# A gated pair of 3x3 convolutions on TensorE's four row groups: contiguous runs of 57 columns a slot, nine-slot blocks, and a new order of visits

## The reference

```python
def qconv_cg(x, w, theta):
    base = cin // 4
    yp = conv3x3(x[:, :base], w[:, :base])
    yr = conv3x3(x[:, base:], w[:, base:])
    d = sigmoid(2.0 * (yp - theta))
    return yp + d * yr
h = relu(bn(qconv_cg(x, w_a, theta_a), ...a))
h = bn(qconv_cg(h, w_b, theta_b), ...b)
return relu(x + h)
```

## Time and profile before

| | |
|---|---|
| median of 3 runs | 467.6 us (467.1 to 467.66) |
| the profiled execution's own time | 467.52 us |
| its span, first to last instruction | 465.7 us |
| TensorE busy | 452.9 us (97%) |
| VectorE, ScalarE busy | 256.0 us (55%), 222.1 us (48%) |
| matmuls | 8233, 8208 of them L323 |

### The profile page before, as it was taken

The page is one execution under the profiler, slowest core; times in us unless marked ns, Lnnn a source line. Parts: engine busy times, 40 slices in busy tenths (PEclk is TensorE's granted clock), DMA queues, the critical chain, the costliest instruction groups (busy, mean ns, idle before and its releaser), DMA issues.

```text
span 465.7 us, 17751 instructions
## 1 busy us (share of the span) xinstructions
PE 452.9 (97%) x8233; PEld 444.1 (95%) x8233; DVE 256.0 (55%) x423; ACT 222.1 (48%) x348; POOL 6.9 (1%) x20
## 2 busy tenths in 40 slices
PE   4999999999999999999999999999999999999994
PEld 4899999999999999999999999999999999999993
DVE  6316655565655565555656565555555565555553
ACT  5226645454544545454544444454545454434332
POOL 5000000000000000000000000000000000000000
PEclk9999999999999999999999999999999999999997
DMA  9930000801526051080605342080333003012315
GB/s 166 219 57 1 4 4 1 140 3 30 114 43 100 4 121 21 4 141 6 136 3 99 45 98 45 3 140 3 67 76 65 9 3 72 1 23 51 72 37 104
DMA packets 116394, 27.13 MB, mean 58 GB/s; under 512 B 116192, under 2 KB 116192, under 8 KB 116320
## 3 DMA queue, kind: packets, MB, share of 16 engines
q1 hardware_dynamic: 115408, 25.86, 30.1%
q10 hardware_dynamic: 592, 0.13, 0.1%
q0 software_dynamic: 320, 0.00, 0.0%
HBM read 13.14 MB, written 12.85 MB: 56 GB/s over the span
## 4 chain that ended last, share of the span: by engine, by line
PE 95%; DMA 2%; ACT 1%; DVE 1%; issue 0%; ACTq 0%
PE acc L323 94%; DMA out_dram<-rows_out 1%; PE acc L287 1%; DMA w_nat<-in_L_conv_w_a_dram 1%; DVE rows_out L545 0%; ACT rows_out L441 0%; ACT L422 0%; ACT mix L422 0%; DVE w_pad L460 0%; ACT w_hi L380 0%; DVE mix L524 0%; ACT x_hi L395 0%; DVE w_pad L458 0%; ACTq L414 0%
## 5 line engine op out<-in xcount | busy, mean ns | idle before, releaser
L323 PE MATMUL acc<-h_hi,w_hi 32*128 32x448 f32 x1392 | 226.7, 367 | 0.0
L323 PE MATMUL acc<-h_lo,w_hi 32*128 32x448 f32 x1392 | 226.6, 367 | 0.0
L323 PE MATMUL acc<-h_hi,w_lo 32*128 32x448 f32 x1392 | 226.5, 367 | 0.0
L323 PE MATMUL acc<-x_hi,w_hi 32*128 32x448 f32 x1344 | 224.4, 374 | 0.8 <-ACT w_hi L380 0.8
L323 PE MATMUL acc<-x_lo,w_hi 32*128 32x448 f32 x1344 | 224.0, 373 | 0.0
L323 PE MATMUL acc<-x_hi,w_lo 32*128 32x448 f32 x1344 | 223.9, 373 | 0.0
L323 PEld LDWEIGHTS acc<-h_hi,w_hi 32*128 32x128 f32 x1392 | 188.3, 184 | 1.2
L323 PEld LDWEIGHTS acc<-h_hi,w_lo 32*128 32x128 f32 x1392 | 188.2, 183 | 1.2
L323 PEld LDWEIGHTS acc<-h_lo,w_hi 32*128 32x128 f32 x1392 | 188.2, 183 | 1.0
L323 PEld LDWEIGHTS acc<-x_hi,w_hi 32*128 32x128 f32 x1344 | 185.5, 188 | 2.7 <-ACT x_hi L395 1.4
L323 PEld LDWEIGHTS acc<-x_hi,w_lo 32*128 32x128 f32 x1344 | 185.8, 188 | 1.3
(11 more groups left out here) (48 smaller groups left out, 30.3 us busy)
## 6 DMA issues: line engine op xcount, KB each, us to landing
x<-in_x_dram SPq DMA_DIRECT2D x30, 392.0 KB, 5.6
out_dram<-rows_out SPq DMA_DIRECT2D x30, 392.0 KB, 6.8
out_dram<-rows_out SPq DMA_DIRECT2D x5, 112.0 KB, 2.5
x<-in_x_dram SPq DMA_DIRECT2D x1, 280.0 KB, 4.8
x<-in_x_dram SPq DMA_DIRECT2D x1, 266.0 KB, 5.5
w_nat<-in_L_conv_w_a_dram SPq DMA_DIRECT2D x1, 144.0 KB, 3.0
w_nat<-in_L_conv_w_b_dram SPq DMA_DIRECT2D x1, 144.0 KB, 4.5
x<-in_x_dram ACTq DMA_DIRECT2D x1, 126.0 KB, 3.1
```

Source lines behind the costliest of these rows:

```text
L323: return pe.matmul(psum[:, bank, 0:N], w[g * ROWS:(g + 1) * ROWS, tap], moving(blk, part, c, dx, g), start=(u == 0 and g in (0, 1)), stop= ...
```

## The change

The moving tiles get a pitch of 57 (`PITCH`): one column of zeros stands between two slots and serves both. A matmul then reads one contiguous run over all slots of its block, the zero columns with it, and their sums are left unread in PSUM. An 8-slot block has 456 columns (`leading` 1), a 9-slot block 512 (`leading` 0, a bank). An a block that takes four slots of each of two images has two runs of 228. The b blocks have nine slots, 12 of them and one of eight slots for each ring of four images, so there are 52 b blocks, 48 with nine slots. Total: 108 blocks.

The order of visits is new. Four blocks are a round; groups 1, 2 and 3 go through its blocks in different turns (`TURNS`) and start 0, 6 and 12 steps after each other, group 0 starts 20 steps after group 1 (`OFFSET`). The first group in a block waits for the inputs and the bank, each later one for the group before it in that block (`group_before`, `visit_done`). There are 18 x 108 + 20 = 1964 steps. ScalarE and VectorE no longer do one block after another but a written order over the round. A b block goes at least eight places (`MARGIN`) behind the a block it needs, as long as a blocks are left; `order` begins with nine a blocks and ends with eight b blocks. The transposes of layer b's weights come before step 13 and those of the parameters before step 16, and six chunks of `x` are split before the loop instead of four.

```diff
-BLK = 8
+BLK, BLK_B = 8, 9
 YR_BANKS, YP_BANKS = 5, 3
-LAG = (42, 0, 21, 42)
+ROUND = 4
+TURNS = ((0, 1, 2, 3), (0, 3, 2, 1), (1, 0, 3, 2), (2, 1, 0, 3))
+OFFSET = (20, 0, 6, 12)
+FIRST_GROUP = (1, 2, 3, 1)
+LAST_GROUP = (3, 1, 2, 3)
 XH_IMGS, X_IMGS, H_IMGS, OUT_IMGS, MIX = 4, 6, 4, 2, 4
-AHEAD = 4
+MARGIN = 8
+AHEAD, SOON = 6, 4
...
-    PADW = W + 2
-    N = BLK * W
+    PITCH = W + 1
     HALF = BLK // 2
...
-    NA, NB = B // 2 * A_PAIR, B * XS // BLK
-    LEAD = A_PAIR
-    order = [("a", n) for n in range(LEAD)]
-    for n in range(max(NA - LEAD, NB)):
-        if n < NB:
...
+    NA = B // 2 * A_PAIR
+    b_blocks = [(ring * HRING + t, min(BLK_B, HRING - t))
+                for ring in range(B // H_IMGS) for t in range(0, HRING, BLK_B)]
+    NB = len(b_blocks)
...
+    order, place = [], {}
+    for n in range(NA + NB):
+        na = sum(kind == "a" for kind, m in order)
+        nb = len(order) - na
+        ready = nb < NB and na >= a_needed(nb) and place["a", a_needed(nb) - 1] + MARGIN <= n
+        blk = ("b", nb) if na == NA or ready and order[-1][0] == "a" else ("a", na)
+        place[blk] = n
+        order.append(blk)
+    TOTAL = len(order)
+    assert TOTAL % ROUND == 0
...
+    def visits(g, b):
+        return b // ROUND * ROUND + TURNS[g].index(b % ROUND) + 1
+    def group_before(g, b):
+        if g in (0, FIRST_GROUP[b % ROUND]):
+            return None
+        return g - 1 if g > 1 else GROUPS - 1
...
+    def slots_of(blk):
+        kind, n = blk
+        return b_blocks[n][1] if kind == "b" else BLK
+    def leading(blk):
+        return 0 if slots_of(blk) == BLK_B else 1
...
-        x_hi = sb("x_hi", [P, XH_IMGS, XS, PADW], F32R)
-        x_lo = sb("x_lo", [P, XH_IMGS, XS, PADW], F32R)
-        h_hi = sb("h_hi", [P, HRING + 1, PADW], F32R)
-        h_lo = sb("h_lo", [P, HRING + 1, PADW], F32R)
-        mix = sb("mix", [P, MIX, N])
+        x_hi = sb("x_hi", [P, XH_IMGS, 1 + XS * PITCH + 1], F32R)
+        x_lo = sb("x_lo", [P, XH_IMGS, 1 + XS * PITCH + 1], F32R)
+        h_hi = sb("h_hi", [P, 1 + (HRING + 1) * PITCH + 1], F32R)
+        h_lo = sb("h_lo", [P, 1 + (HRING + 1) * PITCH + 1], F32R)
+        mix = sb("mix", [P, MIX, BLK_B * W])
...
+        def rows_of(bank, blk):
+            first, k = bank * BANK, slots_of(blk)
+            if leading(blk):
+                at = psum_flat[:, first:first + k * PITCH]
+            elif bank:
+                at = psum_flat[:, first - 1:first - 1 + k * PITCH]
+            else:
+                return psum_flat[:, 0:k * PITCH].rearrange("p (s w) -> p s w", w=PITCH)[:, :, :W]
+            return at.rearrange("p (s w) -> p s w", w=PITCH)[:, :, 1:]
...
-                nc.gpsimd.memset(t[:, :, 0:PADW:PADW - 1].bitcast(F32), 0.0).then_inc(hpads_zero, 1)
+                nc.gpsimd.memset(t[:, 0:1].bitcast(F32), 0.0)
+                nc.gpsimd.memset(t[:, 1::PITCH].bitcast(F32), 0.0).then_inc(hpads_zero, 1)
...
                 kind, n = blk
                 rows = slice(g * ROWS, (g + 1) * ROWS)
+                back = 1 - leading(blk)
                 if kind == "a":
                     tile = (x_hi, x_lo)[part]
                     parts = a_slots(n)
                     img, s, k = parts[0]
-                    at = img % XH_IMGS
+                    at = back + (s + c) * PITCH + dx
                     if len(parts) == 1:
-                        return tile[rows, at, s + c:s + c + k, dx:dx + W]
-                    return tile[rows, at:at + 2, s + c:s + c + k, dx:dx + W]
-                tile = (h_hi, h_lo)[part]
-                t = BLK * n % HRING
-                if t == HRING - HALF:
-                    halves = tile[rows, c:c + HRING].rearrange("p (a b) w -> p a b w", b=HALF)
-                    return halves[:, 0::HRING // HALF - 1, :, dx:dx + W]
-                return tile[rows, t + c:t + c + BLK, dx:dx + W]
+                        return tile[rows, img % XH_IMGS, at:at + k * PITCH]
+                    return tile[rows, img % XH_IMGS:img % XH_IMGS + 2, at:at + k * PITCH]
+                t, k = b_blocks[n]
+                at = back + (t % HRING + c) * PITCH + dx
+                return (h_hi, h_lo)[part][rows, at:at + k * PITCH - back]
+            def sums(bank, blk):
+                kind, n = blk
+                to = psum[:, bank, 0:slots_of(blk) * PITCH - 1 + leading(blk)]
+                if kind == "a" and len(a_slots(n)) == 2:
+                    return to.rearrange("p (i w) -> p i w", i=2)
...
-                return pe.matmul(psum[:, bank, 0:N], w[g * ROWS:(g + 1) * ROWS, tap],
+                alone = g == 0
+                return pe.matmul(sums(bank, blk), w[g * ROWS:(g + 1) * ROWS, tap],
                                  moving(blk, part, c, dx, g),
-                                 start=(u == 0 and g in (0, 1)), stop=(u == UNITS - 1 and g in (0, 3)))
-            for step in range(UNITS * TOTAL + max(LAG)):
-                if step == UNITS:
-                    weights(1, 3)
-                if step == UNITS + 2 * TAPS:
+                                 start=(u == 0 and (alone or g == FIRST_GROUP[b % ROUND])),
+                                 stop=(u == UNITS - 1 and (alone or g == LAST_GROUP[b % ROUND])))
+            for step in range(UNITS * TOTAL + max(OFFSET)):
+                if step == 13:
+                    pe.wait_ge(wlo_ready, 2)
+                    weights(1, 6)
+                if step == 16:
                     pe.wait_ge(prmdup_ready, 2)
                     pe.transpose(psum[:, 5, 0:10], prm_dup[:].rearrange("n c q -> n (c q)"),
                                  ident[0:10, 0:10]).then_inc(prmT_ready, 1)
                 for g in (1, 2, 3, 0):
-                    if not 0 <= step - LAG[g] < UNITS * TOTAL:
+                    if not 0 <= step - OFFSET[g] < UNITS * TOTAL:
                         continue
-                    b, u = divmod(step - LAG[g], UNITS)
+                    visit, u = divmod(step - OFFSET[g], UNITS)
+                    b = visit // ROUND * ROUND + TURNS[g][visit % ROUND]
                     kind, n = order[b]
-                    if g == 1 and u == 0:
...
-                                pe.wait_ge(whi_ready, 4)
-                                pe.wait_ge(wlo_ready, 4)
                         if b >= YR_BANKS:
                             pe.wait_ge(gated_ready, b - YR_BANKS + 1)
...
-                    if g in (2, 3) and u == 0:
-                        pe.wait_ge(tile_done[g - 1], b + 1)
+                    if u == 0 and group_before(g, b):
+                        pe.wait_ge(visit_done[group_before(g, b)], visits(group_before(g, b), b))
                     if g == 0 and u == 0 and b >= YP_BANKS:
                         pe.wait_ge(mixed_ready, b - YP_BANKS + 1)
-                    if g == 1 and u == 0 and b in (3, 4):
+                    if g == 0 and u == 0 and b == 0:
+                        pe.wait_ge(rvar_ready, 1)
+                    if g == 0 and u == 0 and b == 1:
                         pe.wait_ge(whi_ready, 4)
                         pe.wait_ge(wlo_ready, 4)
-                    if g == 0 and u == 0 and b == 0:
-                        pe.wait_ge(rvar_ready, 1)
                     mm = unit(g, b, u)
                     if u == UNITS - 1:
-                        mm.then_inc((yp_ready, tile_done[1], tile_done[2], yr_ready)[g], 1)
+                        mm.then_inc(visit_done[g], 1)
...
-            for n in range(1, AHEAD):
+            for n in range(1, SOON):
                 split_hi(*chunk_of(n))
-            weights_hi(1, 3)
+            weights_hi(1, 6)
             act.wait_ge(rvar_ready, 2)
             nc.scalar.activation(rstd0[:], rvar[:], ACT.Sqrt).then_inc(rstd0_ready, 1)
+            for n in range(SOON, AHEAD):
+                split_hi(*chunk_of(n))
             act.wait_ge(consts_ready, 1)
...
+            for b in range(0, TOTAL, ROUND):
+                gate(b)
+                split_ahead(b)
+                gate(b + 1)
+                split_ahead(b + 1)
+                finish(b)
+                gate(b + 2)
+                finish(b + 1)
+                finish(b + 2)
+                split_ahead(b + 2)
+                gate(b + 3)
+                finish(b + 3)
+                split_ahead(b + 3)
...
+            for b in range(0, TOTAL, ROUND):
+                split_ahead(b)
+                mix_sums(b)
+                split_ahead(b + 1)
+                mix_sums(b + 1)
+                low_parts(b)
+                mix_sums(b + 2)
+                low_parts(b + 1)
+                low_parts(b + 2)
+                split_ahead(b + 2)
+                mix_sums(b + 3)
+                low_parts(b + 3)
+                split_ahead(b + 3)
```

More of the change, by code:

```diff
@@ L514, in _, with mix_sums @@
                 nc.vector.tensor_copy(prm_dup[:, :, q], prm_rows[:]).then_inc(prmdup_ready, 1)
-            for n in range(1, AHEAD):
+            for n in range(1, SOON):
                 split_lo(*chunk_of(n))
-            weights_lo(1, 3)
```

(37 more changed lines are left out.)

141 lines of the change are left out of this document (61 added, 80 removed).

## The result

The changed kernel takes 455.98 us (median of 4 runs, 455.21 to 456.26), the kernel before 467.35 beside it (4 runs, 466.98 to 467.66). The ratio is 0.9754, interval 0.9737 to 0.9771: 11.4 us less, where 37.6 less was forecast. The profiled execution took 456.05 us, with a span of 454.2.

A forecast was written before the change was run, and what follows sets the result against it. TensorE bounds the kernel: steps times pace, plus start and tail. 7.4 + 8.0 start + 399.3 steps + 6.0 waits + 0.2 latency + 6.9 tail = 427.8, plus 1.8 outside the span: 429.6 us; range 422 to 465.

The forecast's parts named there:

- Steps, columns: TensorE's loop: 2094 steps become 1964; groups run freely, so the mean of 480.9 columns counts, 0.2004 us a step.
- The rival in step: TensorE's loop: each step lasts as its widest matmul, 512 columns nearly always; 444 us in all, chance 0.09.
- What a contiguous matmul carries: Cost of each TensorE matmul beyond its columns: 2.9 ns, between bounds 0 and 23.6, giving 0.2033 us a step.
- The text's own sign of being wrong: TensorE's matmul spacing: the prediction is wrong if 480 columns take over 0.21 us, or waits exceed 0.5 us a round.
- The low level shows no cost: Argument for 2.9 ns: at 1.2 GHz matmuls take only their columns, so the extra cost looks like feeding restarted each run.
- the cost is per matmul: Rival on TensorE's pace: the 23.6 ns is paid once per matmul, a step is 0.2240 us; 463 us, chance 0.14.
- Part of the 23.6 stays: Rival on TensorE's pace: another floor of a group's stream leaves some 12 ns a matmul; 441 us, chance 0.22.
- Waits inside a round: Faster steps make group 1 wait for a bank at a round's fourth block: 0.2 to 0.3 us a round, 6 us.
- Start: Before the loop's full pace: clock rises at 21.9 us, so the start loses 8.0 us, against 10.5 before.
- Tail: After TensorE's last unit: 6.9 us of sigmoid, VectorE, ReLU and store, unchanged because the last block keeps eight slots.
- PSUM reads at pitch 57: VectorE's reads of PSUM in rows of 56 with gaps: expected near 0.62 and 0.68 us, no slower for the gaps.
- the slower rival: Gapped PSUM reads lengthen the round's chain: each 0.1 us more costs 13 us, double length gives 510 us; chance 0.08.

The follow-up runs named there:

- the first bench: Matmuls alone, no layer computed, operand form varied by stretch; a group's starts lie 206.7 ns apart for float32r 448 in one run, 189.2 for bf16.
- the bench: Matmuls alone, float32r, several pitches, then 512 columns with and without other engines working: 226.7 ns each, 228.9 with each group's columns shifted.

## Why the prediction was wrong, point by point

**Steps, columns: right.** 1964 steps, and groups that keep each its own pace. The mean of columns is the one that counts; with the units above the mean is (60 x 208.9 + 48 x 231.4)/108 = 218.9 ns. The rival in step is refuted by the rows at 409.38 to 409.90, and by the step of 0.2206, since 512 columns and 18 ns in nearly every step would make 0.229. The Trainium skill's rule that matmuls start in program order (TensorE: Matmul & The Clock Gate, "The mechanism") doesn't hold for the starts of different row groups in this trace. For what the semaphores say it does; see the last section.

**"What a contiguous matmul carries": this step failed.** It took 2.9 ns, one run's share of 23.6; the measured value is 18.5. 1964 times the missing 15.6 is 30.6 us, and 429.6 + 30.6 = 460.2. The terms below (4 less in waits, 1.7 less at the start, 1.4 more in the tail) make it 455.9. The bounds (0 to 23.6) held it, and so did the wide range (422 to 465); the choice of 2.9 between the bounds didn't, nor did the forecast's own range (423 to 437), whose cost per matmul ended at 5 ns. The text's own sign of being wrong, 480 columns in over 0.21, came true. Two arguments carried the choice. "The low level shows no cost" was true, but a cost once per float32r matmul vanishes at that level too (in the first bench one group alone, 448 columns in one run at the 1.2 GHz level, has 373.3 ns, its columns and nothing more), so it told nothing of runs. And the one shape in the trace was read as eight equal runs, when nothing there varied the number of runs. What is there instead: 16 to 20 ns for each float32r matmul of 448 columns, 2.5 for bf16, and a few ns for where the rows start. The nearest rival, in mechanism and in time, was "the cost is per matmul", with 23.6 ns, 463 us and a chance of 0.14; with 18.5 it gives 1964 x 5.1 = 10 us less, 453, and the waits of 2 us that its slower step had ruled out. "Part of the 23.6 stays" (12 ns, 441 us, 0.22) lies 15 us off. The Trainium skill's gap of about 2.5 ns beyond the columns (the same page, "Back-to-back issue gap") fits bf16 here (189.2 for 448 columns, 2.5 beyond them) and not float32r (206.7, 20.0 beyond).

**Waits inside a round: wrong in size, and in place.** 6.0 us forecast. The text had said that above 0.213 a step the waits go; with 0.2189 about 2 remain, as 0.2206 against 0.2195 shows. Per round they are 0.08 us at the start of group 0's fourth block, which the text had called just in time, and 0.05 for groups 1 to 3, inside or at the start of the first block of their round; group 1 loses nothing at the start of its fourth block, where the 0.2 to 0.3 had been put.

**Start: right, and a little better.** Loss forecast 8.0, against 10.5 before; measured 6.3. That is what the other terms leave of TensorE's stretch (445.94 - 0.2 - 7.56 - 429.9 - 2), but a count gives the same: by 50 us group 1 has begun 172 units, 162 of them of 456 columns, worth 36.2 us at their paces, and 50 - 7.56 - 36.2 = 6.3. The high level came at 19.55, not 21.9.

**Tail: 1.4 us short.** 6.9 was carried over as unchanged, since the last block keeps eight slots; but four blocks now end nearly together and queue on VectorE.

**PSUM reads at pitch 57: right.** 644, 642 and 647 ns for (60 x 448 + 48 x 504)/108 = 473 elements on average, beside 621 and 634 for 448: the slower rival is refuted.

The sum with measured terms: 7.6 + 6.3 + 429.9 + 2 + 0.2 + 8.3 + 1.8 = 456.1, against 456.05 profiled. What tests it is the start counted at 50 us; taken as the remainder, it would make the sum agree by itself.

Where the gain of 11.4 us comes from, by kernels that differ in one part: pitch 57 gives 4.3 with runs (0.9909) and 5.5 with rows (0.9882); the nine-slot blocks with the new start's transposes, on top of the runs, 1.7; the new order 5.2. The nine-slot blocks cut the fixed 18.5 ns to fewer matmuls, but 512 columns carry it too.

**Open.** Why a float32r matmul pays this once, and not by columns, was not found; in one run it is 20 ns at 448 columns and 13.3 to 13.4 at 256, 384 and 512, so it isn't one number either. In the kernel 512 columns take 231.4, alone 226.7; other engines are excluded, and the groups' different addresses give 2.2 of it in the bench, which is an indication, not a proof.

## What to carry to other kernels

Before the shape of an operand is redesigned to save a cost per matmul, measure the spacing with the shape and the type varied one at a time: a trace with one shape can't say whether a fixed cost belongs to the run, the matmul or the type. With float32r split in three products, the low-order ones in bf16 save more than any layout tried here. When an order of visits is changed, count both ends: matmuls begun by a fixed time for the start, and how many blocks become whole together at the end.
